# Second attention of a two-layer GNN/MoE kernel: ring buffers for the edge lists, the largest score by TensorE and VectorE, and the next stage's row statistics inside it

## The chip, the cores and the metric

One core of a Trainium2 chip runs the whole program. The metric is the device time of one execution in microseconds; the median of several runs is given. The engines are named as in the profile: PE (TensorE matmuls), PEld (its weight loads), DVE (VectorE), ACT (ScalarE), POOL (GpSimd) and SP (SyncE, here only a queue that issues DMAs). Each engine runs its own program; they meet at semaphores.

## The reference

x is 6250 rows of 256 columns, and there are 100,000 edges (src, dst) sorted by dst. Four stages add to x in turn, each on a layernorm of x:

```python
x = x + _L0_gnn_ref(_layernorm(x), edge_index, ...)      # first attention, one edge for each row
x = x + _L0_ffn_ref(_layernorm(x)[None], ...)[0]         # MoE, 6 experts, top 2
x = x + _L1_gnn_ref(_layernorm(x), edge_index, ...)      # second attention (GAT), 4 heads of 64
x = x + _L1_ffn_ref(_layernorm(x)[None], ...)[0]         # MoE, 8 experts, hidden 1024, top 2
```

The second attention, where most of the change is, computes for every edge and self-loop

```python
h = (x @ W).reshape(n, HEADS, OUT_C)
e = a_src[src] + a_dst[dst]
e = jnp.where(e > 0, e, NEG_SLOPE * e)
ex = jnp.exp(e - m[dst])                       # m: largest e of the destination
alpha = ex / (segment_sum(ex, dst)[dst] + 1e-16)
out = relu(segment_sum(alpha[:, :, None] * h[src], dst) + bias)
```

The kernel subtracts a bound instead of m: leaky_relu(largest a_src of all rows + a_dst of the row), which gives the same quotient. The second MoE's gate takes logits of the normalized rows, the two largest of 8, and a softmax over the two.

## The kernel before

The 6250 rows are 49 tiles of 128 (`TILES`), and x stays in SBUF (`K.X`). The stages follow each other, each in its own Blocks (a Block starts and ends with a barrier of all engines):

- `project` with tag a1: layernorm, first attention's part and router of the first MoE; its tokens are scattered into slots, 7 trips of 7 tiles (`TRIPS`, `BODY`). It stands at 100 to 420 us. A stage e0 computes the first MoE's experts, and b0, again `project`, combines and projects h and the scores for the second attention (`K.AD` holds a_src and a_dst of every row, `K.T1` in DRAM the rows h and a_src).
- `attention`: 865 to 2429 us.
- `project` with `gate`, tag b1: 2429 to 2627 us. Per trip of 7 tiles: `update` makes bn_stats (L793) and bn_aggr (L797) on DVE; `deviations` Sqrt on ACT (L926); `norm` the reciprocal and seven scalings (L812); PE transposes (L993), ACT copies (L959, L962), PE logits (L1004); `place` on DVE finds the two experts and, with PE's counts (`count`, L1026 to L1031, `ranks`), the slots (L860 to L880); POOL scatters 14 times into the slots (L691). POOL fills `token` and a column of `pad` with iota (L668, L670) at its start, and DVE copies the tokens (L737).
- e1, the second MoE's experts, to the end.

**The attention.** A first Block takes the largest a_src: DVE reduces over tiles (L1594 to L1597), POOL over partitions (`partition_all_reduce`, L1610), DVE makes the bound `adm` and the self-loops' exponents (L1599 to L1605), ACT takes Exp (L1615). The second Block walks 49 tiles of destinations; each has one or more steps of 17 x 128 = 2176 edges, some fifty steps in all, numbered s. A step's edges are three groups j of 6, 6 and 5 chunks of 128 (`CHUNKS`). For each group:

- SP loads the sources (`idx[j]`, L1685) once `scored[j]` says that DVE has used the gathered rows, and the destinations (`dcol[j]`, L1687) once `onehots[j]` is up; one load of `own` per tile (L1676). Loads of 24 or 20 bytes for each partition; the order on SP is idx0, dcol0, idx1, dcol1, idx2, dcol2.
- POOL waits for `src_in[j]` and for `agg_done[j]` of the step before, then issues one indirect gather for each chunk (L1700) of 128 rows into `G[j]`: 6, 6, 5 instructions.
- DVE compares the destinations with the tile's numbers: one-hots `OH[j]` (L1711). PE turns them (`turn`, L1836), ACT copies them to SBUF (`keep_turned`, L1809), PE multiplies them by the destinations' scores (`destinations`, L1844), DVE adds and rectifies (`scores`, L1720 to L1724), ACT takes Exp twice (`exps`, L1815, L1816), DVE weighs the rows (`weigh`, L1731), PE sums them into the tile (`aggregate`, L1851, `agg_done[j]`).

The order on each engine is written out. PE in a step: turn 0, turn 1, destinations 0, 1, (wait `acc_done`), aggregate 0, turn 2, destinations 2, aggregate 1, aggregate 2. ACT: keep_turned 0, 1, exps 0, keep_turned 2, exps 1, exps 2. DVE: one_hots 0, 1, scores 0, weigh 0, `absorb` of the step before (L1749), at a tile's end `finalize` (L1753 to L1760: divide, bias, relu, add to x), start of the next ACC (L1775, L1778), one_hots 2, scores 1, weigh 1, scores 2, weigh 2.

`lift` raises a semaphore by one at the start, so that `freed(eng, sem, n)`, a wait for n+1, passes for the first use. `Chain` is DVE's own order: `link` waits for the instruction before, `mark` only counts, `settle` waits for all.

## Time and profile before

| | us |
|---|---|
| runs | 3304.72, 3318.38, 3322.56 |
| median | 3318.38 |
| profiled execution | 3312.67, its span 3310.6 |
| second attention, share of the span | 1547 (47%) |
| b1 | 198 (6%) |
| a1, e0 with b0, e1 | 320, 440, 683 |
| busy over the span: PE, DVE, POOL, ACT | 2159, 1549, 1487, 1006 |
| mean granted clock of PE | 0.77 |

A profile row of a timeline gives the start in us from the span's start, the busy time, engine, line and operation, the tiles written and read, and in brackets the engine's idle time before it with what ended that. "remote" is an event whose origin the trace doesn't name, "issue" none that it shows. Busy time of POOL for an indirect DMA is the issuing; the transfer goes on behind it. The times of PE's ends are modelled. The column of rows named waits sums idle time by what ended it: total, number, longest.

### The profile page before, as it was taken

How to read it: one execution, taken by the hardware profiler on the slowest of the kernel's cores; microseconds unless marked ns; L12 is line 12 of the kernel's file. 1: busy time of each engine (PE TensorE's matmuls, PEld its weight loads, DVE VectorE, ACT ScalarE, POOL GpSimd, SP SyncE). 2: the span in 40 equal slices, each digit the busy share in tenths (PEclk: the TensorE clock that was granted, in tenths of full speed). 3: DMA queues.
4: the chain of work that ended last, by engine and by line, in shares of the span. 5: the costliest groups of instructions: out<-in, count | busy, mean ns of one | idle time of the engine just before them, and what ended most of it. 6: DMA issues, size and time to landing. Idle time of an engine off the chain costs nothing. (4 is left out here: it accounts for less than half of the span.)

```text
span 3310.6 us, 55683 instructions
## 1 busy us (share of the span) xinstructions
PE 2158.7 (65%) x13130; PEld 1965.5 (59%) x13131; DVE 1548.6 (47%) x4163; ACT 1006.1 (30%) x2712; POOL 1486.7 (45%) x1459
## 2 busy tenths in 40 slices
PE   6232259984466655656755656655654299999997
PEld 4132258873355554555654555555543299999997
DVE  5564435657334433433433433433445345556454
ACT  3132246663210111111111111111134266665664
POOL 1456634440255555555555545545525524334233
PEclk9655579997667767766767767767755599999999
DMA  6212233325333233233223323323333423333331
GB/s 177 62 55 66 73 114 106 110 93 188 93 82 78 76 79 79 76 79 78 76 79 78 79 73 79 79 77 80 79 98 125 137 42 89 46 66 85 48 68 25
DMA packets 232367, 279.34 MB, mean 84 GB/s; under 512 B 102963, under 2 KB 186526, under 8 KB 232086
## 3 DMA queue, kind: packets, MB, share of 16 engines
q0 software_dynamic: 82160, 200.19, 22.9%
q1 hardware_dynamic: 149392, 77.86, 9.0%
q10 hardware_dynamic: 776, 0.89, 0.1%
q14 instruction: 30, 0.25, 0.0%
q8 instruction: 9, 0.15, 0.0%
HBM read 202.11 MB, written 78.46 MB: 85 GB/s over the span
## 5 line engine op out<-in xcount | busy, mean ns | idle before, releaser
L1700 POOL DMA_INDIRECT at_G<-h_as,at_idx x850 | 805.9, 948 | 735.2 <-issue 385.5
L1851 PE MATMUL at_pAgg<-at_G,at_OH 128*128 128x260 f32 x1700 | 504.6, 462 | 91.8 <-DVE at_ACC L1749 51.0
L1851 PEld LDWEIGHTS at_pAgg<-at_G,at_OH 128*128 128x128 f32 x1700 | 387.6, 235 | 176.6 <-issue 51.3
L1836 PE MATMUL at_pTr<-g_ident,at_OH 128*128 128x128 f32 x850 | 157.1, 332 | 477.7 <-ACT at_OT L1809 436.9
L1809 ACT ACTIVATE at_OT<-at_pTr 128x384 f32<-128x384 f32 (+1 forms) x300 | 131.4, 471 | 1102.8 <-remote 695.3
L1836 PEld LDWEIGHTS at_pTr<-g_ident,at_OH 128*128 128x128 f32 x850 | 120.9, 170 | 513.7 <-ACT at_OT L1809 448.7
L1415 ACT ACTIVATE e_full<-e_pH,g_bias_hidden 128x256 f32<-128x256 f32 x640 | 322.6, 504 | 96.4 <-PE e_pH L1320 60.7
L1223 POOL DMA_INDIRECT out_dram<-e_ob,e_to x108 | 171.0, 1584 | 401.9 <-DMA out_dram<-e_ob,e_to 190.8
L1844 PEld LDWEIGHTS at_pAd<-at_cur,at_OT 128*128 128x128 f32 x1700 | 320.4, 290 | 49.8 <-ACT at_OT L1809 49.8
L1720 DVE TENSOR_TENSOR at_Z<-at_G,at_pAd 128x24 f32<-128x24 f32 x150 | 26.1, 174 | 690.0 <-PE at_pAd L1844 592.0
L1844 PE MATMUL at_pAd<-at_cur,at_OT 128*128 128x8 f32 x1700 | 319.1, 326 | 37.9 <-ACT at_OT L1809 37.9
L1731 DVE TENSOR_TENSOR at_G<-at_G,at_pIds 128x1536 f32<-128x1536 f32 x150 | 249.8, 1666 | 151.4 <-ACT at_pIds L1816 97.2
L1318 PE MATMUL e_pH<-e_xT_high,e_WA_high 128*128 128x256 f32 x1072 | 308.8, 288 | 7.6 <-DVE e_WA_low L1491 4.8
L1496 DVE TENSOR_TENSOR e_hT_low<-e_full,e_hT_high 128x256 fp32r<-128x256 f32 x536 | 260.0, 498 | 108.9 <-ACT e_hT_high L1416 107.4
L1319 PE MATMUL e_pH<-e_xT_low,e_WA_high 128*128 128x256 f32 x1072 | 303.3, 283 | 0.0
L1320 PE MATMUL e_pH<-e_xT_high,e_WA_low 128*128 128x256 f32 x1072 | 303.0, 283 | 0.0
L1416 ACT ACTIVATE e_hT_high<-e_pH,g_bias_hidden 128x256 fp32r<-128x256 f32 x536 | 275.3, 514 | 0.0
L1318 PE MATMUL e_pO<-e_WL_high,e_hT_high 128*128 128x256 f32 x864 | 250.0, 289 | 5.2 <-POOL e_WL_low L1247 3.4
L1319 PE MATMUL e_pO<-e_WL_low,e_hT_high 128*128 128x256 f32 x864 | 244.1, 283 | 0.0
L1320 PE MATMUL e_pO<-e_WL_high,e_hT_low 128*128 128x256 f32 x864 | 243.9, 282 | 0.0
L1318 PEld LDWEIGHTS e_pH<-e_xT_high,e_WA_high 128*128 128x128 f32 x1072 | 204.0, 190 | 12.1 <-issue 8.5
L1319 PEld LDWEIGHTS e_pH<-e_xT_low,e_WA_high 128*128 128x128 f32 x1072 | 204.5, 191 | 0.0
(307 smaller groups left out, 4089.3 us busy)
## 6 DMA issues: line engine op xcount, KB each, us to landing
e_xs<-slot_rows_e SPq DMA_DIRECT2D x55, 261.0 KB
e_xs<-slot_rows_e SPq DMA_DIRECT2D x54, 257.0 KB
at_G<-h_as,at_idx POOLq DMA_INDIRECT x850
b_rows<-expert_out SPq DMA_DIRECT2D x14, 896.0 KB, 7.3
g_raw_first<-in_L_ffn_W_dram POOLq DMA_DIRECT2D x8, 1024.0 KB, 8.1
g_raw_last<-in_L_ffn_W_dram POOLq DMA_DIRECT2D x8, 1024.0 KB, 6.3
xt_ar<-a_og SPq DMA_DIRECT2D x7, 910.0 KB, 4.5
h_as<-b_og SPq DMA_DIRECT2D x7, 910.0 KB
```

The source lines that it names most:

```text
L1223: gp.indirect_dma_start(K.out, at, ob[b][:, s, :], None, bounds_check=NODES - 1, oob_is_err=False, compute_op=ALU.add).then_inc(sent[s], 16)
L1318: nc.tensor.matmul(out, left[0], right[0], start=start, stop=False)
L1319: nc.tensor.matmul(out, left[0], right[1], start=False, stop=False)
L1320: return nc.tensor.matmul(out, left[1], right[0], start=False, stop=stop)
L1415: nc.scalar.activation(full[n][:, :], pH[n][:, 0:MT], func, bias=at)
L1416: nc.scalar.activation(to[b][0][:, u, :], pH[n][:, 0:MT], func, bias=at).then_inc(h_done, 1)
L1496: V.tensor_tensor(to[b][1][:, u, :], full[base + u % RING][:, :], to[b][0][:, u, :], ALU.subtract).then_inc(l_done, 1)
L1700: gp.indirect_dma_start(G[j][:, c, :], None, K.T1, bass.IndirectOffsetOnAxis(ap=idx[j][:, c:c + 1], axis=0)).then_inc(gathered[j], 16)
L1731: V.tensor_tensor(rows, rows, ex, ALU.mult).then_inc(msg_ready, 1)
L1836: last = nc.tensor.transpose(pTr[h][:, (c - a) * P:(c - a + 1) * P], OH[j][:, c, :], K.ident[:, :])
L1844: last = nc.tensor.matmul(pAd[j][:, 8 * c:8 * c + 8], OT[j][:, c, :], cur[:, :], start=True, stop=True)
L1851: last = nc.tensor.matmul(pAgg[:, 0:DIM + 4], OH[j][:, c, :], G[j][:, c, :], start=(j == 0 and c == 0), stop=(j == NJ - 1 and c == CHUNKS[ ...
```

## The change

1. **Attention.** The two Blocks become one. The maximum over partitions is made without POOL: PE turns `gm` (128 x 4), DVE reduces it to four numbers (`top`) and spreads them on a 4 x 4 diagonal (`each`), PE multiplies a matrix of ones by it, DVE copies the result. `maxima()` runs on DVE ahead of tile 0, ACT takes the self-loops' Exp in the same Block. Edge lists: one load for sources and one for destinations for each step (68 bytes for each partition, all 17 chunks) into rings of four steps (`edge_src`, `edge_dst`, `DEPTH`); SP waits for the slot to be free, and for both loads to land before the next step. `own` is a ring of four as well. ACT copies a group's sources from the ring to `idx[j]` (`keep_sources`), behind `exps(s, j)` for the next step, and POOL waits for `src_kept[j]` in place of `src_in[j]`. DVE reads the destinations from the ring. `finalize` also makes bn_stats and bn_aggr of the finished rows and keeps mean and variance of all tiles in `K.MV`.
2. **b1.** `update` does nothing; one Sqrt and one reciprocal over all 49 tiles stand at the start, and `norm` reads `K.MV` and `rstd` by tile.
3. **a1 and b1.** POOL's two iotas go; tokens are made once at the kernel's setup (`K.token`), and DVE derives the pad column.

```diff
 @@ project @@
-                nc.gpsimd.iota(token[:, :], pattern=[[P, TILES]], base=0, channel_multiplier=1,
-                               allow_small_or_imprecise_dtypes=True).then_inc(token_made, 1)
...
-                    v.wait_ge(token_made, 1)
-                    nc.vector.tensor_copy(Y[:, :, TO], token[:, :]).then_inc(consts, 1)
-
+                    nc.vector.tensor_copy(Y[:, :, TO], K.token[:, :]).then_inc(consts, 1)
...
                 def update(i):
 
+                    if gate:
+                        return
...
-                    v.wait_ge(std_ready, i + 1)
-                    nc.vector.reciprocal(rstd[:, :, :], std[:, :, :]).then_inc(rstd_ready, 1)
-                    v.wait_ge(rstd_ready, i + 1)
+                    if not gate or (isinstance(i, int) and i == 0):
+                        v.wait_ge(std_ready, i + 1)
+                        nc.vector.reciprocal(rstd[:, :, :], std[:, :, :]).then_inc(rstd_ready, 1)
+                        v.wait_ge(rstd_ready, i + 1)
...
-                        if j == BODY - 2:
+                        if j == BODY - 2 and not gate:
 @@ attention, SP @@
-                            freed(sp, scored[j], s)
-                            sp.dma_start(idx[j][:, :], K.SRCP[bass.ds(at[j], ne)].rearrange("(p c) -> p c", p=P)).then_inc(src_in[j], 16)
-                            freed(sp, onehots[j], s)
-                            sp.dma_start(dcol[j][:, :], K.DSTP[bass.ds(at[j], ne)].rearrange("(p c) -> p c", p=P)).then_inc(dst_in[j], 16)
+                        slot = sp.snap(s % DEPTH)
+                        landed = sp.snap(s * 16 + 16)
+                        sp.wait_ge(src_kept[NJ - 1], s + 1)
+                        sp.sem_inc(passed, 1)
+                        sp.dma_start(edge_src[:, bass.ds(slot, 1), :].rearrange("p o c -> p (o c)"),
+                                     K.SRCP[bass.ds(e0, SE)].rearrange("(p c) -> p c", p=P)).then_inc(src_in, 16)
+                        sp.wait_ge(onehots[NJ - 1], s + 1)
+                        sp.sem_inc(passed, 1)
+                        sp.dma_start(edge_dst[:, bass.ds(slot, 1), :].rearrange("p o c -> p (o c)"),
+                                     K.DSTP[bass.ds(e0, SE)].rearrange("(p c) -> p c", p=P)).then_inc(dst_in, 16)
+                        sp.wait_ge(src_in, landed)
+                        sp.wait_ge(dst_in, landed)
+                        sp.sem_inc(passed, 1)
 @@ attention, POOL @@
-                        gp.wait_ge(src_in[j], s * 16 + 16)
+                        gp.wait_ge(src_kept[j], s + (1 + (DEPTH if j == NJ - 1 else 0)))
                         freed(gp, agg_done[j], s)
 @@ attention, DVE: finalize @@
-                    ch.mark(V.scalar_tensor_tensor(Xt, res[:, :], 0.0, Xt, ALU.max, ALU.add))
+                    ch.link(V.scalar_tensor_tensor(Xt, res[:, :], 0.0, Xt, ALU.max, ALU.add))
+                    v.sem_inc(passed, 1)
+                    ch.link(V.bn_stats(stats[:, :], Xt))
+                    v.sem_inc(passed, 1)
+                    ch.link(V.bn_aggr(mean_var[:, :], stats[:, :]))
+                    ch.mark(V.tensor_copy(K.MV[:, bass.ds(t, 1), :].rearrange("p o k -> p (o k)"), mean_var[:, :]))
 @@ attention, DVE: maxima @@
+                    V.tensor_tensor(gm[:, :], gm[:, :], gt[:, :], ALU.max).then_inc(gm_ready, 1)
+                    v.wait_ge(gm_turned, 1)
+                    ch.link(V.tensor_reduce(top[:, :], pAgg[0:HEADS, 0:P], AX.X, ALU.max))
+                    V.tensor_scalar(each[:, :], K.ident[0:HEADS, 0:HEADS], top[:, 0:1], None, ALU.mult).then_inc(each_ready, 1)
+                    v.wait_ge(gm_all, 1)
+                    ch.link(V.tensor_copy(gt[:, :], pAgg[:, P:P + HEADS]))
 @@ attention, ACT @@
+                for j in J:
+                    keep_sources(0, j)
+                act.wait_ge(self_z, 1)
+                nc.scalar.activation(exs[:, :, :], exs[:, :, :], ACT.Exp).then_inc(exs_ready, 1)
...
                     keep_turned(s, 0)
                     keep_turned(s, 1)
                     exps(s, 0)
+                    keep_sources(ahead, 0)
                     keep_turned(s, 2)
                     exps(s, 1)
+                    keep_sources(ahead, 1)
                     exps(s, 2)
+                    keep_sources(ahead, 2)
 @@ attention, PE @@
+                pe.wait_ge(gm_ready, 1)
+                nc.tensor.transpose(pAgg[0:HEADS, 0:P], gm[:, :], K.ident[:, :]).then_inc(gm_turned, 1)
+                pe.wait_ge(each_ready, 1)
+                nc.tensor.matmul(pAgg[:, P:P + HEADS], allones[:, :], each[:, :], start=True, stop=True).then_inc(gm_all, 1)
```

`keep_sources(s, j)` waits for `src_in` of the step and is one ACT copy of 6 or 5 columns from the ring to `idx[j]`.

## Rows read from the trace of the kernel before

**Rows 1.** Windows by stage: us, busy (instructions) of PE, PEld, DVE, ACT, POOL, clock, DMA, GB/s.

```profile
882.00:2429.00 1547.00, 960.29 (x4250) 827.56 (x4248) 622.42 (x1388) 171.27 (x600) 805.06 (x850) 0.71 0.30 78
2429.00:2627.00 198.00, 67.56 (x351) 60.65 (x351) 84.35 (x403) 62.28 (x133) 96.83 (x102) 0.50 0.40 127
```

**Rows 2.** Waits in 1000 to 2200 us: total, times, longest.

```profile
ACT at_OT L1809 <- remote: 542.2, 41, 14.4
...
POOL at_G L1700 <- DMA at_idx<-src_padded: 162.6, 23, 7.4
POOL at_G L1700 <- PE at_pAgg L1851: 111.7, 15, 11.3
```

**Rows 3.** Timeline of one attention step, from one first gather to the next.

```profile
1029.67 0.95 POOL L1700 DMA_INDIRECT at_G<-h_as,at_idx  x1 [7.05 <-PE at_pAgg L1851]
...
1031.95 5.09 PE L1851 MATMUL at_pAgg<-at_G,at_OH 128*128 128x260 f32 x22 [0.70 <-DVE at_G L1731]
...
1037.30 0.87 PE L1836 MATMUL at_pTr<-g_ident,at_OH 128*128 128x128 f32 x6 [0.26 <-issue]
...
1043.44 0.94 POOL L1700 DMA_INDIRECT at_G<-h_as,at_idx  x1 [0.30 <-issue]
1046.73 0.87 ACT L1809 ACTIVATE at_OT<-at_pTr 128x384 f32<-128x384 f32 x2 [13.79 <-remote]
...
1047.45 0.94 POOL L1700 DMA_INDIRECT at_G<-h_as,at_idx  x1 [3.06 <-issue]
...
1054.74 4.79 PE L1851 MATMUL at_pAgg<-at_G,at_OH 128*128 128x260 f32 x12 [1.00 <-DVE at_ACC L1749]
...
1057.15 0.82 DVE L1711 TENSOR_TENSOR at_OH<-at_dcol,at_pIds 128x640 f32<-128x640 f32 x1 [0.22 <-DVE at_ACC L1778]
...
1059.37 0.71 PE L1836 MATMUL at_pTr<-g_ident,at_OH 128*128 128x128 f32 x5
...
1060.37 0.95 POOL L1700 DMA_INDIRECT at_G<-h_as,at_idx  x1 [6.97 <-PE at_pAgg L1851]
```

**Rows 4.** Timeline of the attention's start.

```profile
871.65 0.26 DVE L1599 COPY at_adm<-g_as_ad 128x196 f32<-128x196 f32 x1 [5.26 <-POOL at_gt L1610]
...
874.88 0.29 DVE L1791 TENSOR_SCALAR at_pIds<-g_iota 128x128 f32<-128x128 f32 x1 [0.69 <-PEq L1588]
...
881.19 1.19 POOL L1700 DMA_INDIRECT at_G<-h_as,at_idx  x1 [9.58 <-issue]
...
905.32 0.77 ACT L1809 ACTIVATE at_OT<-at_pTr 128x384 f32<-128x384 f32 x2 [13.54 <-remote]
```

**Rows 5.** Timeline of b1's start.

```profile
2429.22 1.28 ACT L926 ACT_TABLE_LOAD   x1 [6.64 <-PEq L1667]
...
2437.75 0.21 DVE L737 COPY b_Y<-b_token 128x49 f32<-128x49 f32 x1 [7.30 <-POOL b_token L668]
...
2438.14 2.39 DVE L793 BATCH_NORM_STATS2 b_stats<-g_x 128x6 f32<-128x256 f32 x7
...
2440.68 0.58 DVE L797 BATCH_NORM_AGGREGATE b_mv<-b_stats 128x2 f32<-128x6 f32 x7 [0.15 <-DVE b_stats L793]
...
2441.87 2.35 DVE L812 TENSOR_SCALAR b_yg<-g_x,b_mv,b_rstd 128x256 f32<-128x256 f32 x7
...
2450.93 1.28 ACT L959 ACT_TABLE_LOAD   x1
```

**Rows 6.** Timeline of b1's loop, second and last stream of scatters.

```profile
2483.24 0.22 DVE L860 TENSOR_TENSOR b_rank<-b_pr,b_region 128x56 f32<-128x56 f32 x1 [8.18 <-remote]
...
2486.59 0.97 POOL L691 DMA_INDIRECT slot_rows_e<-b_Y,g_slot_of  x1 [5.51 <-DVE g_slot_of L880]
...
2491.95 2.38 DVE L812 TENSOR_SCALAR b_yg<-g_x,b_mv,b_rstd 128x256 f32 x7 [1.99 <-issue]
...
2584.72 0.22 DVE L860 TENSOR_TENSOR b_rank<-b_pr,b_region 128x56 f32<-128x56 f32 x1 [0.55 <-PE b_pr L1031]
```

**Rows 7.** Timeline of POOL in a1: the scatter behind a pair of trips.

```profile
272.50 0.99 POOL L691 DMA_INDIRECT slot_rows_e<-a_Y,g_slot_of  x1 [7.04 <-DVE g_slot_of L880]
```

More of the change, by code:

```diff
@@ L41 @@
 CHUNKS = (6, 6, 5)
-OFFS = (0, 6 * P, 12 * P)
+OFFS = (0, 6, 12)
+ALL = sum(CHUNKS)
+DEPTH = 4
 SE = sum(CHUNKS) * P
@@ L397, in project @@
         stats = sb("stats", [P, BODY, 6])
-        mv = sb("mv", [P, BODY, 2])
-        std = sb("std", [P, BODY, 1])
-        rstd = sb("rstd", [P, BODY, 1])
+        n_std = TILES if gate else BODY
+        mv = K.MV if gate else sb("mv", [P, BODY, 2])
+        std = sb("std", [P, n_std, 1])
+        rstd = sb("rstd", [P, n_std, 1])
         yg = sb("yg", [P, BODY, DIM])
@@ L733, in _ @@
                         for e in range(2):
-                            last = nc.vector.memset(pad[:, e, :, part], 0.0)
-                    last.then_inc(pad_made, 1)
-                    v.wait_ge(token_made, 1)
-                    nc.vector.tensor_copy(Y[:, :, TO], token[:, :]).then_inc(consts, 1)
+                            nc.vector.memset(pad[:, e, :, part], 0.0)
+                    nc.vector.tensor_scalar(pad[:, :, :, TO].rearrange("p e s -> p (e s)"), K.token[:, 0:2 * SUB],
+                                            float(2 * NODEROWS if router else NODEROWS), None, ALU.add).then_inc(pad_made, 1)
+                    nc.vector.tensor_copy(Y[:, :, TO], K.token[:, :]).then_inc(consts, 1)
                     nc.vector.tensor_scalar(rev[:, :], K.iota[:, 0:E], -1.0, float(E), ALU.mult, ALU.add).then_inc(consts, 1)
@@ L924, in deviations @@
                         nc.scalar.activation(z[:, :, :], z[:, :, :], ACT.Exp).then_inc(exps_done, 1)
-                    act.wait_ge(stats_ready, i + 1)
+                    if not gate:
+                        act.wait_ge(stats_ready, i + 1)
                     nc.scalar.activation(std[:, :, :], mv[:, :, 1:2], ACT.Sqrt, bias=K.eps[:, 0:1]).then_inc(std_ready, 1)
@@ L1581, in attention @@
         gt = sb("gt", [P, HEADS])
+        top = sb("top", [HEADS, 1])
+        each = sb("each", [HEADS, HEADS])
+        allones = sb("allones", [HEADS, P])
         adm = sb("adm", [P, TILES, 8])
@@ L1622, in attention @@
         Z = [sb(f"Z{j}", [P, CHUNKS[j], HEADS]) for j in J]
-        own = sb("own", [P, DIM + 4])
+        own = sb("own", [P, DEPTH, DIM + 4])
         cur = sb("cur", [P, 8])
@@ L1657, in attention @@
         NJ = len(CHUNKS)
-        lifts = (own_used, acc_done, ot_ready, *scored, *onehots, *agg_done)
-        START, STEP, END = 2, 3 * NJ, 5
+        lifts = (acc_done, ot_ready, *scored, *onehots[0:NJ - 1], *agg_done)
+        START, STEP, END = 2, 3 * NJ, 8
+        stats = sb("stats", [P, 6])
+        mean_var = sb("mean_var", [P, 2])
         def tile_steps(eng, t):
@@ L1772, in tile @@
                         finalize(ch, t - 1)
+                    own_t = own[:, bass.ds(t % DEPTH if isinstance(t, int) else v.snap(t % DEPTH), 1), 0:DIM].rearrange("p o c -> p (o c)")
                     ex_t = exs[:, bass.ds(t, 1), :].rearrange("p o h -> p (o h)")
@@ L1789, in tile @@
                             assert cs.n == STEP
+                v.sem_inc(own_used, DEPTH)
+                v.sem_inc(onehots[NJ - 1], DEPTH)
+                maxima()
                 V.tensor_scalar(TI, K.iota[:, 0:P], -float(P), None, ALU.add).then_inc(init, 1)
@@ L1817, in exps, with keep_sources @@
                                          ACT.Exp).then_inc(ex_ready, 1)
+                def keep_sources(s, j):
+                    slot = act.snap(s % DEPTH) if not isinstance(s, int) else s % DEPTH
+                    act.wait_ge(src_in, s * 16 + 16)
+                    act.sem_inc(passed, 1)
+                    nc.scalar.activation(idx[j][:, :], edge_src[:, bass.ds(slot, 1), OFFS[j]:OFFS[j] + CHUNKS[j]].rearrange("p o c -> p (o c)"),
+                                         ACT.Copy).then_inc(src_kept[j], 1)
+                act.sem_inc(src_kept[NJ - 1], DEPTH)
+                for j in J:
+                    keep_sources(0, j)
+                act.wait_ge(self_z, 1)
+                nc.scalar.activation(exs[:, :, :], exs[:, :, :], ACT.Exp).then_inc(exs_ready, 1)
                 n, s0 = tile_steps(act, TILES - 1)
-                with act.Fori(0, act.snap(s0 + n)) as s:
+                total = act.snap(s0 + n)
+                with act.Fori(0, total) as s:
+                    ahead = act.snap(s + 1)
                     keep_turned(s, 0)
@@ L1830, in turn @@
                 def turn(s, j):
-                    freed(pe, onehots[j], s + 1)
+                    pe.wait_ge(onehots[j], s + (2 if j < NJ - 1 else 1 + DEPTH))
                     for h, (a, z) in enumerate(((0, 3), (3, CHUNKS[j]))):
```

102 lines of the change are left out of this document (54 added, 48 removed).

## The prediction

> **What bounds the kernel now.** I read the windows by stage first. The second attention takes 1547 of 3310 us, and in it no engine is full: PE 960, POOL 805, DVE 622, ACT 171 us [rows 1]. So a loop of waits bounds it, and the next view is the list of waits over forty of its steps [rows 2]. The largest entry is ACT's: 41 waits of 13 us each for "remote" in front of the OT copy. POOL's own long pauses are 23 that end with the index load (162.6 us) and 15 with PE's aggregation (111.7 us).
>
> The timeline of one step tells what lies behind them [rows 3]. POOL issues twelve gathers (groups 0 and 1), the last at 1043.44 for 0.94. PE ended the transposes that ACT wants at 1037.30+0.87=1038.17, yet ACT's OT copy starts only at 1046.73: 8.6 us after PE's end and 2.35 us after POOL's stream. POOL goes on with group 2 at 1047.45, also for something that PE had long ended. So **PE's completions reach nobody while POOL streams software DMAs**, from some 7 us into a stream until 2.3 us after it. In the stream of five that follows, handovers are prompt. From the release the path runs: ACT 1046.73, PE, DVE's scores and weighing, PE's aggregation of group 0 from 1054.74 to 1059.53, POOL's gather of the next step at 1060.37. Twelve gathers of 1.25 and the tail of 2.3 (17 us) bring the next release. The first gathers of two steps stand at 1029.67 and 1060.37, 30.70 us apart; fifty such steps are the stage.
>
> The gate and projection in front of the second MoE (b1, 198 us [rows 1]) has the same trait: POOL scatters 14 at a time by 1.27 us, DVE's rank addition L860 at 2483.24 waits 8.18 us for "remote", and the next scatter is at 2486.59 after a pause of 5.51 [rows 6].
>
> **The change part by part.** The sum is made against the profiled run, 3312.67 us (span 3310.6 and 2.1 around it); the median of the runs is 5.7 above it.
>
> (1) *Maximum without POOL, one Block instead of two.* Before, DVE idles 5.26 us for POOL's reduction; the second Block's first DVE instruction is at 874.88, the first gather 6.3 later at 881.19 [rows 4]. After, the index load starts with the Block (865.6) and needs nothing of DVE: 865.6+6.3, and 0.6 for ACT's copy, is 872.5, nearly 9 earlier. But the seven additions (0.36 to 0.40 each in the old order) and two handovers through PE bring DVE to the first one-hots some 3.5 us after the gathers. PE's first aggregation then falls over 7 us into a first stream of 17 gathers (21 us), and is likely held to its end, as ACT's wait of 13.54 us at 905.32, in this very step, was [rows 4]. So of the 9 us some 5 are given back. I take -4; bounds -9 (nothing held) and +3 (all of step 0 behind the stream).
>
> (2) *Rings of four, one load for three.* SP's waits for `scored` and `onehots` leave the path of the indices; ACT, busy 171 of 1547 us [rows 1], copies them. The tempting reading is that the 23 pauses that end with the index load go. They don't: with the load named a pause is 162.6/23=7.07 us, with PE named, its longest taken out, (111.7-11.3)/14=7.17 us [rows 2]. Both conditions come true within a few tenths of each other. PE's aggregation ends 0.84 before the gather, and POOL needed 0.72 from a release (ACT's start at 1046.73) to its gather at 1047.45 [rows 3]: what is late next is PE, by 0.1 to 0.2 us. I take 0.15 us for 48 steps and 3 for the one long pause: -10. Bounds 0, and 0.5 for each step, -25. Half of the index descriptors go, but no row shows a full DMA queue: nothing for it. Slots modulo four cost register steps on SP, ACT and DVE; DVE's are counted in (3).
>
> (3) *Row statistics in `finalize`, once per tile.* One more link behind L1760, bn_stats of 256 columns (2.39/7=0.34), bn_aggr (0.58/7=0.08 in a row of seven [rows 5]; linked about 0.2, an estimate from DVE's small operations) and a copy of 0.17, with semaphores and slot arithmetic: 1.1 us (0.8 to 1.5). Queued behind them on DVE are ACC's start, group 2's one-hots (1057.15+0.82=1057.97) and group 1's scores. PE turns group 2 at 1059.37, behind its twelve aggregation matmuls [rows 3], so 1.2 to 1.4 us are free: cost nothing, 49 times. If that cover is gone, PE's groups 1 and 2 come later, and behind them lie the 9 us in which results are held anyway. Only the last tile pays in the open: +0.8 at the stage's end.
>
> (4) *b1's start.* DVE waits 7.30 us for POOL's iota, then makes 2.39+0.58 of statistics; after ACT's Sqrt norm starts at 2441.87 [rows 5]. After the change nothing of POOL is in front: ACT's table load from 2429.22 to 2430.50, one Sqrt of 49 columns, a reciprocal, norm at about 2431.5: -10.4. In trip 0 ACT's detour (a table load of 1.28, a Sqrt of 0.3, and the load back at 2450.93 [rows 5]) goes too: -2.9. The first scatter comes 13.3 earlier; with (3)'s 0.8 taken off, -12.5. Bounds -9 (the gate's weights or bias land last) and -14.
>
> (5) *b1's loop.* Without statistics norm begins about 0.6 instead of 5.4 us into a stream of scatters (2491.95 against 2486.59 [rows 6]), and the count's matmuls about 7.2 us into it. The last trip shows what may be had: it has no norm ahead, L860 goes at 2584.72, 7.3 us into its stream, after 0.55 us of waiting [rows 6], and POOL scatters 28 without a pause. If each trip does so, five pauses of 5.0 to 5.5 us go: -26. But 7.2 is just where holding begins, and in a stream that runs on, transposes and logits of the next trip are held as well. The first router stage shows what comes then: two trips merged into one stream and a pause of 7.04 behind the pair [rows 7]. Five pauses of 5.3 against three of some 6.2: -8. Bounds 0 and -26.
>
> (6) *Iotas of a1 and setup.* Setup makes the tokens once, beside loads; in a1 DVE, not POOL's first gather, is late. Nothing.
>
> Sum: -4 -10 -12.5 -8 = -34.5, 3278 on the profiled run. The runs' median is 5.7 higher, of which I carry most: **3282 us**.
>
> Two rules of the Trainium skill are against this. GPSIMD Engine Reference, 4.1 Engine selection, gives a reduction along the partition dimension to GPSIMD and not to VectorE; by it, part (1) would cost its two handovers through PE, +1 instead of -4, and the total would be 3287. The wait of 5.26 us in front of L1599 speaks against the rule for one reduction of four columns. SBUF — State Buffer, Who interferes with whom, says that PE and ACT never wait on anyone and that DMA does not contend with a compute engine; ACT's 13.79 us for results that were complete 8.6 us before speaks of something that the page doesn't treat. By that rule part (5) would give its whole -26, total 3264.
>
> **The rivals.**
> *A, the label at its face*: the index load is what POOL waits for; in 49 steps 29 pauses of 7.07 us vanish, -205: 3087. Against it stands the equal length of the pauses that end with PE. 3%.
> *B, the rhythm flips*: group 1's aggregation ends about 5.2 us into the stream of twelve (12 of the 22 matmuls from 1031.95 [rows 3]). If its completion is held, POOL stops after six gathers, so the hold ends early (7.5+2.3), and it resumes with eleven; 13.7 us from that release to the next step, less what overlaps, makes a step of about 27.1: -3.6 for 49 steps, 3106. By the rows it takes 2 to 3 us of delay on DVE (L860 passed at 7.3, the transposes at 8.5 were held); I allow for one, and (3) adds 1.1 against 1.2 of slack. 9%.
> *C, b1 scatters without pauses*: -18 more, 3264. 22%.
> *D, little happens*: (1) gives +3, (2) and (5) nothing, (4) stays: -10, 3308 on the median. All three sit at the edge of the held time. 15%.
> *E, slower*: the statistics land on the path. The place is DVE between absorb L1749 and group 2's one-hots; from 1.2 us of added work on, PE's turn of group 2 and its aggregation of groups 1 and 2 move, and if the held time doesn't take this up, each tile pays what was added, 1.1 us, up to 1.9 with one more handover (0.8): 49 times, +54 to +93, 3336 to 3375. Against it: ACT's copies of group 2 and the next step's work come before a release that POOL alone sets. 8%.
> *F, the rings never run ahead*, since SP waits for both loads of a step before the next: (2) is nought, all else as forecast, 3292.
>
> **How the numbers follow.** The forecast has 43%, F among it, C 22, D 15, B 9, A 3, E 8. The range leaves out A, B and E, 20%: from C with (1) and (2) at better values (3264-5-15=3244, taken 3240) to D's 3308 with its rounding, 3312. A measurement of this kernel can tell about 0.5% (16.6 us) from no change. Faster: forecast, C, A, B, 0.77; same, D, 0.15; slower, E, 0.08.
>
> **What would show it.** In the new profile the first gathers of two steps stand 30.5 to 30.6 us apart (B: 27; E: over 31.5); POOL's pause before them is about 6.9 with PE named each time; ACT's waits of 13 to 14 us for "remote" are still there; PE's turn of group 2 still follows its twelve matmuls at once. The first gather is at 872 to 873, the second step's near 904. b1's first scatter comes 13 us sooner after attention's end, no Sqrt load stands in its loop, and POOL pauses fewer than five times. The prediction is wrong if a step's length changes by over 0.5 us either way, the only term with a factor of fifty.

## The result and the profile after

| | before | after |
|---|---|---|
| median of 6 runs each, us | 3315.3 | 3219.0 |
| range | 3304.7 to 3322.6 | 3203.9 to 3238.0 |
| profiled run, its span | 3312.7, 3310.6 | 3223.0, 3221.4 |
| mean granted clock of PE | 0.77 | 0.773 |

The ratio is 0.972, 95% interval 0.970 to 0.974: 96 us faster. The forecast was 3282, range 3240 to 3312; the direction was right and the gain nearly three times what was forecast.

Windows by stage of the changed kernel, in the columns of [rows 1]: second attention, then b1.

```profile
869.40:2353.20 1483.80, 1008.46 (x4250) 842.39 (x4250) 673.63 (x1539) 194.32 (x752) 813.83 (x850) 0.71 0.30 81
2353.20:2537.20 184.00, 67.81 (x351) 60.29 (x351) 62.62 (x300) 43.93 (x114) 98.04 (x100) 0.50 0.45 137
```

Attention takes 1484 us (869.4, its first gather, to 2353.2) and does the same work: POOL 814 us busy against 805. The 89 us between the two spans split as follows. The start of attention, read at the first gather of its second step, gives 4.4 (906.06 to 901.65). From there to the first gather of the last step it was 1482.8 us and is 1404.7: 78.1. The last step and the stage's end cost 6.6. The way from attention's end to b1's first scatter went from 34.3 to 22.3 us: 12.0. b1's scatters give 3.4, and what lies between them and e1 costs 2. So nearly all of the surprise is in the 48 steps between the second and the last, of 30.9 us before and 29.3 on average now.

Before, they were nearly equal (47 of 48 take 30.5 to 31.5 us). That is no longer so. Timeline of the changed kernel over two steps: the last of SP's loads first, then POOL's first gather of each pause and the work that answers to [rows 3] (turn is L1890, OT copy L1845, aggregation L1905).

```profile
1016.41 0.35 SPq L1662 DMA_DIRECT2D at_own<-h_as  x1
1017.40 0.34 SPq L1671 DMA_DIRECT2D at_edge_src<-src_padded  x1
...
1017.60 0.95 POOL L1701 DMA_INDIRECT at_G<-h_as,at_idx  x1 [11.12 <-PE at_pAgg L1905]
...
1020.73 5.09 PE L1905 MATMUL at_pAgg<-at_G,at_OH 128*128 128x260 f32 x22 [0.70 <-DVE at_G L1735]
...
1026.99 0.95 POOL L1701 DMA_INDIRECT at_G<-h_as,at_idx  x1 [2.13 <-issue]
...
1042.71 0.77 ACT L1845 ACTIVATE at_OT<-at_pTr 128x384 f32<-128x384 f32 x2 [11.69 <-remote]
...
1043.43 0.96 POOL L1701 DMA_INDIRECT at_G<-h_as,at_idx  x1 [2.88 <-issue]
...
1045.68 7.08 PE L1905 MATMUL at_pAgg<-at_G,at_OH 128*128 128x260 f32 x22
...
1051.37 0.95 POOL L1701 DMA_INDIRECT at_G<-h_as,at_idx  x1 [0.68 <-issue]
...
1060.56 0.87 ACT L1845 ACTIVATE at_OT<-at_pTr 128x384 f32<-128x384 f32 x2 [13.20 <-remote]
...
1068.15 0.42 DVE L1753 TENSOR_TENSOR at_ACC<-at_ACC,at_pAgg 128x260 f32<-128x260 f32 x1
...
1072.85 0.82 DVE L1715 TENSOR_TENSOR at_OH<-at_edge_dst,at_pIds 128x640 f32<-128x640 f32 x1 [0.30 <-DVE at_ACC L1811]
...
1074.84 0.95 POOL L1701 DMA_INDIRECT at_G<-h_as,at_idx  x1 [7.46 <-PE at_pAgg L1905]
```

The first step runs from 1017.60 to 1043.43, **25.8 us**. POOL stops after six gathers of group 0 (at +7.3) and waits 2.13 us, until +9.4. Group 1's aggregation was ready to tell by +6 (12 of the 22 matmuls from 1020.73), but reaches POOL only once POOL's stream has ended. In that pause everything PE held comes through, ACT and PE go on at once, and groups 1 and 2 follow as one stream of eleven. At its end, 2.2 us later, the OT copy (1042.71) and group 0's aggregation are released together, and the next step's gathers start at 1043.43 without the 7 us that stood there before. The second step, from 1043.43 to 1074.84, is of the old kind (31.4): group 1 is told of at +7.9, POOL idles 0.68, the stream of twelve runs to 1058.6, ACT waits for its end, and the pause of 7.46 before the next first gather is back. Of 48 steps 22 are short (25.9 us on average), 14 take 29 to 32 us and 12 take 33 to 35. Only 6 of the 26 long ones are of the old kind, at 31 to 32 us.

The other 20, from 28.6 to 35.0 us, are a third kind. POOL's first gathers of groups 0, 1, 2 in the last step of the changed kernel:

```profile
2306.39 0.95 POOL L1701 DMA_INDIRECT at_G<-h_as,at_idx  x1 [12.22 <-PE at_pAgg L1905]
...
2314.33 0.95 POOL L1701 DMA_INDIRECT at_G<-h_as,at_idx  x1 [0.68 <-issue]
...
2322.18 0.96 POOL L1701 DMA_INDIRECT at_G<-h_as,at_idx  x1 [0.59 <-issue]
```

Here group 2 found its condition true in the middle of the stream (pause 0.59), POOL ran 17 gathers with no rest of even 1 us, and all that PE owed the other engines came late. The step before it, from 2272.41, has the same pauses (0.62 and 0.64) and took 34.0 us.

### The profile page after: what moved, and what is told of

Read it like the earlier page. It is cut to its first block and busy times, and to the rows that moved or that the text cites. A ratio compares the mean times of both kernels' runs of the same rounds, so it can differ in the third digit from the quotient of the medians.

```text
span 3221.4 us, 56679 instructions
## 1 busy us (share of the span) xinstructions
PE 2203.0 (68%) x13133; PEld 1975.8 (61%) x13134; DVE 1577.0 (49%) x4212; ACT 1010.1 (31%) x2846; POOL 1493.4 (46%) x1455
## 3 DMA queue, kind: packets, MB, share of 16 engines
q0 software_dynamic: 82160, 200.19, 23.2%
## 5 line engine op out<-in xcount | busy, mean ns | idle before, releaser
L1905 PE MATMUL at_pAgg<-at_G,at_OH 128*128 128x260 f32 x1700 | 592.4, 524 | 154.0 <-DVE at_ACC L1753 84.7
L1905 PEld LDWEIGHTS at_pAgg<-at_G,at_OH 128*128 128x128 f32 x1700 | 448.4, 270 | 260.8 <-DVE at_G L1735 127.7
L1845 ACT ACTIVATE at_OT<-at_pTr 128x384 f32<-128x384 f32 (+1 forms) x300 | 130.4, 471 | 999.0 <-remote 522.4
L1898 PE MATMUL at_pAd<-at_cur,at_OT 128*128 128x8 f32 x1700 | 293.9, 309 | 133.2 <-ACT at_OT L1845 118.3
L1898 PEld LDWEIGHTS at_pAd<-at_cur,at_OT 128*128 128x128 f32 x1700 | 290.2, 264 | 147.1 <-ACT at_OT L1845 130.1
L1890 PE MATMUL at_pTr<-g_ident,at_OH 128*128 128x128 f32 x850 | 144.4, 307 | 188.9 <-ACT at_OT L1845 94.9
L1890 PEld LDWEIGHTS at_pTr<-g_ident,at_OH 128*128 128x128 f32 x850 | 107.0, 156 | 234.0 <-issue 119.9
```

The source lines that it names most:

```text
L1890: last = nc.tensor.transpose(pTr[h][:, (c - a) * P:(c - a + 1) * P], OH[j][:, c, :], K.ident[:, :])
L1898: last = nc.tensor.matmul(pAd[j][:, 8 * c:8 * c + 8], OT[j][:, c, :], cur[:, :], start=True, stop=True)
L1905: last = nc.tensor.matmul(pAgg[:, 0:DIM + 4], OH[j][:, c, :], G[j][:, c, :], start=(j == 0 and c == 0), stop=(j == NJ - 1 and c == CHUNKS[ ...
```

## The experiments

The experiments ran on four chips. On two of them the kernel before takes 3333 us, and PE's completions are held back while POOL streams, as the prediction describes; this is called the hold below. On the two others it takes 2783 us, and the traces show no hold at all. Ratios are always to the kernel before on the same chip. The diffs are excerpts.

**Statistics alone, in the kernel before.**

```diff
-                    ch.mark(V.scalar_tensor_tensor(Xt, res[:, :], 0.0, Xt, ALU.max, ALU.add))
+                    ch.link(V.scalar_tensor_tensor(Xt, res[:, :], 0.0, Xt, ALU.max, ALU.add))
...
+                    ch.link(V.bn_stats(stats[:, :], Xt))
...
+                    ch.link(V.bn_aggr(mean_var[:, :], stats[:, :]))
+                    ch.mark(V.tensor_copy(kept[:, bass.ds(t, 1), :].rearrange("p o k -> p (o k)"), mean_var[:, :]))
```

> The kernel before with one addition: finalize also makes bn_stats, bn_aggr and a copy on DVE for each tile, whose result nobody reads (b1 still makes its own). Theory 1 (the added DVE work shifts group 1's aggregation past the point from which PE's completions are held, POOL then stops after six gathers and the hold ends early): the steps alternate between about 25.9 and 31 to 33 us as in the changed kernel, and the run is 50 to 80 us faster than before although it only has more work. Theory 2 (the rings and the fewer loads make the short steps): steps stay at 30.8 us, the time is that of before plus 0 to 2 us.

Measured: 3408.5 against 3333.4, ratio 1.023 (1.021 to 1.025). Slower, with 45 of 48 steps at 32 to 33 us and no short one. Both theories fall: the statistics alone do not make short steps, and they cost 1.5 us a step. Timeline of one step end:

```profile
1172.54 0.42 DVE L1783 TENSOR_TENSOR at_ACC<-at_own,at_exs 128x256 f32<-128x256 f32 x1
...
1173.15 0.34 SPq L1679 DMA_DIRECT2D at_own<-h_as  x1
...
1173.89 0.33 SPq L1688 DMA_DIRECT2D at_idx<-src_padded  x1
...
1174.24 0.75 PE L1844 MATMUL at_pTr<-g_ident,at_OH 128*128 128x128 f32 x5
...
1176.44 0.94 POOL L1703 DMA_INDIRECT at_G<-h_as,at_idx  x1 [8.41 <-DMA at_idx<-src_padded]
```

ACC's start (L1783) comes behind the statistics; own's load waits for it, the index load stands behind own's load on SP, and POOL's gather waits for the index load, 8.41 us instead of 6.97 [rows 3]. PE's turn of group 2 (1174.24) waits for nothing new.

**The change without its statistics.** `finalize` and b1 as before; rings, maximum and iotas as changed.

> The changed kernel with the statistics taken back to b1 (update, Sqrt and reciprocal for each trip as before); rings, the maximum without POOL and the iotas stay as changed. Theory 1: steps of 30.5 to 30.7 us, and against before only the start of attention (-4), some of the loop (-5 to -10) and b1's start without the iota (-7): 3295 to 3302 where before has 3315. Theory 2: the alternation of 25.9 and 31 to 33 us is still there, about 3235.

Measured: 3177.8 against 3333.4, ratio 0.954 (0.951 to 0.958), on the chip of the first experiment. Theory 1 falls, theory 2 stands: short steps need no statistics, and of the rest of the change only the rings are in the loop. Of 48 steps 32 are short, the mean is 28.1 us. SP's load, then POOL's first gathers, in one of them (the next step begins at 1183.87):

```profile
1156.84 0.01 SPq L1669 DMA_DIRECT2D at_edge_src<-src_padded  x1
...
1157.81 0.95 POOL L1699 DMA_INDIRECT at_G<-h_as,at_idx  x1 [2.87 <-issue]
...
1167.19 0.95 POOL L1699 DMA_INDIRECT at_G<-h_as,at_idx  x1 [2.15 <-issue]
```

**One wait more.** In the changed kernel, and for itself in the kernel before:

```diff
                        freed(gp, agg_done[j], s)
                        gp.sem_inc(passed, 1)
+                        if j == 1:
+                            freed(gp, agg_done[2], s)
+                            gp.sem_inc(passed, 1)
```

> The changed kernel with one wait more: before group 1's gathers POOL waits for group 2's aggregation of the step before as well (it had to wait for it before group 2 anyway). Theory 1: POOL now pauses after six gathers in every step, PE's completions come through there, and the two groups behind it run as one stream of eleven; the short step of 25.9 to 26.5 us becomes the rule, 49 times 2.5 to 3 us less than the changed kernel's mean of 29.2: 3219-130=3090, range 3070 to 3120. Theory 2 and any theory in which a wait costs POOL time: a step is longer by the pause of 1 to 2 us, 3219+50=3270 or more.

> The kernel before with the same one wait more and nothing else of the change. Theory 1: steps of 25.9 to 26.5 us, or up to 0.8 more where the index loads now come last, 49 times 4 to 4.9 less: 3315-220=3095, range 3075 to 3150. Theory 2: as before or slower by 1 to 2 us for each step, 3315 to 3400.

Measured: 3134.9, ratio 0.940 (0.937 to 0.943), and 3144.7, ratio 0.942 (0.940 to 0.945). The added wait alone, without any of the change, is worth 5.8%, more than the change in any of its runs (2.8 to 4.9%). In either kernel nearly every step is 27.3 us; POOL's first gathers in one of the changed kernel:

```profile
1138.40 0.95 POOL L1704 DMA_INDIRECT at_G<-h_as,at_idx  x1 [2.82 <-issue]
...
1149.06 0.95 POOL L1704 DMA_INDIRECT at_G<-h_as,at_idx  x1 [3.41 <-PE at_pAgg L1908]
```

The pause behind the sixth gather is 3.4 us, since group 2's aggregation ends last, and the step ends with a pause of 2.9 (the next one begins at 1165.73) where the old one had 7. The expected 3090 was too low by 45, mainly because group 1 starts at +10.7 and not at +9.4. Since the kernel before, with its own loads, gets the same steps, the pause is enough, whatever SP's loads do.

**Own's ring under the statistics.** The first experiment with own in a ring of four and nothing else of the change (SP's side; DVE reads the same slot):

```diff
-                    freed(sp, own_used, t)
-                    sp.dma_start(own[:, :], K.T1[bass.ds(r0, P), :]).then_inc(own_in, 16)
+                    place = sp.snap(t % 4)
+                    sp.wait_ge(own_used, t + 1)
+                    sp.sem_inc(passed, 1)
+                    sp.dma_start(own[:, bass.ds(place, 1), :].rearrange("p o c -> p (o c)"), K.T1[bass.ds(r0, P), :]).then_inc(own_in, 16)
```

> The kernel before with the unused row statistics of the first experiment and, from the change, only the ring of four for own (so that SP loads own before ACC's start of the tile before has used the last one). In the first experiment the pause before the first gather ended with the index load, which stands on SP behind own's load, which waits for ACC's start, which stands on DVE behind the statistics. Theory P (that chain is what the statistics cost): with the chain cut the 32.4 us steps fall to 30.8 us or below, the time is 3325 to 3340 where before has 3333. Rival Q (the statistics cost by PE's and DVE's work coming later, whatever SP does): steps stay at 32.3 us, about 3408.

This run fell on the chip without the hold: 2786.1 against 2783.3, ratio 1.002 (1.000 to 1.004), steps of 21.4 us. List of waits over 37 of its steps:

```profile
ACT at_OT L1821 <- PE at_pTr L1848: 506.6, 112, 8.5
```

ACT's OT copy waits only for the transposes themselves, no entry names "remote", and POOL's gaps are the 0.30 us between two gathers: 17 gathers of 1.25 us are the step. That chip tells nothing of theory P. The kernel was run again elsewhere:

> As for the run of the same kernel before, which fell on a chip without the hold and so told nothing of it (there ratio 1.002). On a chip with the hold: theory P (the statistics cost because own's load and then the index load stand behind them) 30.8 us steps or less, ratio 0.97 to 1.002; rival Q (they cost by later PE and DVE work) 32.3 us steps, ratio 1.02.

Measured: 3283.3 against 3333.6, ratio 0.986 (0.983 to 0.990). Theory P holds: with the chain through SP cut, the statistics cost nothing, 33 of 48 steps take 30.7 to 31.6 us, and 12 take 26 or 27 us. In 4 of the 12 POOL stops for 2.1 to 2.2 us behind the sixth gather, as in the changed kernel, so such steps also come without the rings of the edge lists. POOL's first gathers around one:

```profile
1094.31 0.94 POOL L1705 DMA_INDIRECT at_G<-h_as,at_idx  x1 [6.83 <-PE at_pAgg L1863]
...
1103.66 0.94 POOL L1705 DMA_INDIRECT at_G<-h_as,at_idx  x1 [2.17 <-issue]
...
1120.25 0.94 POOL L1705 DMA_INDIRECT at_G<-h_as,at_idx  x1 [3.14 <-remote]
```

**A wait for the landed rows.**

```diff
+                        if j == 1:
+                            gp.wait_ge(gathered[0], s * (16 * CHUNKS[0]) + 16 * CHUNKS[0])
+                            gp.sem_inc(passed, 1)
```

> The changed kernel with one other wait: before group 1's gathers POOL waits until its own six gathers of group 0 have landed (about 2 us after the last). Theory 1 (any pause of POOL behind the sixth gather that is long enough to let PE's completions through gives the short step): group 1 starts 9.4 to 9.6 us after the first gather in every step, steps of 26.0 to 26.3 us, 1 us shorter than with the wait for group 2's aggregation, where POOL went on at +10.7: 3135-50=3085 on this count, range 3070 to 3110. Rival R (what helps is that group 2's aggregation is in before group 1 starts, not the pause): the streams of 11 become streams of 11 with a pause or of 17, steps of 29 us and more, 3200 or above.

> As for the run of the same kernel before, which on a chip without the hold made each step 2.4 us longer (23.8 us, ratio 1.036), the price of the pause itself. On a chip with the hold: theory 1, steps of 26.0 to 26.3 us, ratio 0.925; rival R, 29 us and more, ratio 0.965 or above.

On the chip without the hold: 2885.0 against 2783.3, ratio 1.036 (1.034 to 1.038), 23.8 us a step; the pause is pure loss there. On a chip with it: 3097.5 against 3333.6, ratio 0.931 (0.927 to 0.934), steps of 26.5 us:

```profile
1096.26 0.95 POOL L1704 DMA_INDIRECT at_G<-h_as,at_idx  x1 [3.12 <-issue]
...
1106.13 0.96 POOL L1704 DMA_INDIRECT at_G<-h_as,at_idx  x1 [2.62 <-DMA at_G<-h_as,at_idx]
```

This is the fastest version measured on a chip with the hold, 236 us below the kernel before, 96 us (by ratio 0.931 against 0.956) below the changed kernel on the same chip. The next step begins at 1122.76. Theory 1's part on the pause stands, rival R falls.

**SP's loads moved.** The kernel without statistics, with SP's three loads held until DVE has issued group 2's weighing (`v.sem_inc(past, 1)` behind it):

```diff
                    sp.wait_ge(own_used, t + 1)
...
+                    sp.wait_ge(past, s0 + 1)
...
                        sp.wait_ge(src_kept[NJ - 1], s + 1)
...
+                        sp.wait_ge(past, s + 1)
```

> The kernel of the second experiment (rings, no statistics in attention) with SP's three loads of a step (own, sources, destinations) held until DVE has issued the weighing of group 2, so that they are issued about 4 us into the stream or in POOL's pause, not in the 3 us before the first gather. Theory S (loads issued by SP just before the stream make the hold of PE's completions begin early, at 5 to 6 us instead of after 7, and so make the short steps): nearly all steps are 30.6 us, 3178 + 50 x 2.5 = 3300. Rival T (the loads have no part in it; the time at which PE ends group 1's aggregation decides): steps as in the second experiment, 26.0 in most, mean 28.1, about 3180.

> As for the run of the same kernel before (rings, no statistics, SP's loads kept out of the last 3 us before the stream), which fell on a chip without the hold (ratio 0.996). On a chip with the hold: theory S (loads just before the stream make the hold begin early) nearly all steps 30.6 us, ratio 0.99; rival T, steps as in the second experiment, ratio 0.954.

Without the hold: 2771.9, ratio 0.996 (0.994 to 0.998). With it: 3307.6 against 3333.6, ratio 0.991 (0.988 to 0.994), and 45 of 48 steps at 30.7 to 31.4 us. SP's loads and POOL's first gathers in one step:

```profile
1099.96 0.02 SPq L1663 DMA_DIRECT2D at_own<-h_as  x1
1105.02 0.70 SPq L1674 DMA_DIRECT2D at_edge_src<-src_padded  x1
1108.58 0.70 SPq L1678 DMA_DIRECT2D at_edge_dst<-dst_padded  x1
...
1095.79 0.95 POOL L1704 DMA_INDIRECT at_G<-h_as,at_idx  x1 [6.82 <-PE at_pAgg L1905]
...
1113.84 0.95 POOL L1704 DMA_INDIRECT at_G<-h_as,at_idx  x1 [3.25 <-issue]
```

The loads come 4 to 13 us into the stream, and POOL stops only once, before group 2. So SP's loads have a part in the short steps, as theory S said. The experiment alone doesn't exclude rival T, for with late loads PE also ends group 1's aggregation earlier than in most short steps. Steps of the kernel without statistics in which PE keeps the same times decide that:

```profile
1480.52 0.34 SPq L1669 DMA_DIRECT2D at_edge_src<-src_padded  x1
...
1482.28 0.95 POOL L1699 DMA_INDIRECT at_G<-h_as,at_idx  x1 [6.75 <-PE at_pAgg L1898]
...
1484.63 5.09 PE L1898 MATMUL at_pAgg<-at_G,at_OH 128*128 128x260 f32 x22 [0.70 <-DVE at_G L1733]
...
1491.75 0.95 POOL L1699 DMA_INDIRECT at_G<-h_as,at_idx  x1 [2.23 <-issue]
...
2230.03 0.95 POOL L1699 DMA_INDIRECT at_G<-h_as,at_idx  x1 [6.52 <-PE at_pAgg L1898]
...
2232.39 5.09 PE L1898 MATMUL at_pAgg<-at_G,at_OH 128*128 128x260 f32 x22 [0.70 <-DVE at_G L1733]
...
2237.57 0.95 POOL L1699 DMA_INDIRECT at_G<-h_as,at_idx  x1 [0.30 <-issue]
```

In both, PE's aggregation starts 2.4 us after the first gather and takes 5.09. In the first, SP's loads stand 2.8 to 1.2 us before the stream, and POOL waits 2.23 us; in the second there is none in the last 3.5 us, and POOL goes on after 0.30. All four steps of the first kind in this trace were held, all three of the second were not.

But the loads are not the whole trigger. In the changed kernel's trace 22 steps have the sources' load 0.7 to 1.1 us before the stream; in 4 of them POOL waited over 2 us for group 1, in 18 it went on within 1.4 us. The step at 1043.43 above is one of the 18 (its load at 1042.58, pause 0.68). In the kernel with only own's ring the short step at 1094.31 had no load in the 7 us before it. And the kernel before issued its index loads 1.1 to 2.7 us before the first gather and had no short step. Own's load isn't needed: in the step at 1157.81 it stood 6.6 us before the stream. What in the loads does it is open. Two kernels were to tell the edge loads from own's:

> Rings, no statistics, and only the two edge loads of a step held until DVE has issued the weighing of group 2; own's load as in the change. Theory S1 (the edge loads 1 us before the stream make the early hold): steps of 30.7 us in most, ratio 0.985 to 0.995. Rival S2 (own's load does it): short steps stay in more than half, ratio 0.95 to 0.965. On a chip without the hold both give 0.995 to 1.0 and tell nothing.

> Rings, no statistics, and only own's load held until DVE has issued the weighing of group 2; edge loads as in the change, though SP reaches them only behind own's load. Theory S1: as SP then stands in own's wait while the stream begins, the edge loads too come after it, so steps of 30.7 us, ratio 0.985 to 0.995; if they still are 1 us before the stream, short steps and 0.955. Rival S2: 30.7 us steps wherever the edge loads are. The place of the loads in the trace, beside the steps, decides between the two.

Both fell on a chip without the hold (2772.0 and 2772.6 against 2782.7, ratios 0.996 and 0.996) and tell nothing of it.

**Gathers of 16 bytes.** The kernel before, gathering 4 columns in place of 260:

```diff
-                            gp.indirect_dma_start(G[j][:, c, :], None, K.T1,
+                            gp.indirect_dma_start(G[j][:, c, DIM:DIM + 4], None, K.T1.rearrange("n (a b) -> (n a) b", b=4),
...
+                for j in J:
+                    V.memset(G[j][:, :, 0:DIM], 0.0)
```

It leaves the messages out of the attention's result (their columns stay zero), and the index, counted in pieces of 16 bytes, no longer finds the source's scores.

> The kernel before with gathers of 4 columns (16 bytes for each partition) in place of 260; the message columns of G are zeros, so the second attention's sums are left out of the output, and POOL still issues 17 gathers for each step. Theory U (the hold comes from POOL's issuing): ACT's wait of 13 to 14 us for remote and steps of 30 to 31 us stay, time within 30 us of before. Rival V (it comes from the moving of the gathered rows, 133 KB for each gather): the hold is gone, the steps are bound by POOL at 22 to 26 us, time 3333-250 or less.

> The kernel before with gathers of 4 columns instead of 260 (the message columns are zeros, so the second attention's sums are left out), as in the run that fell on a chip without the hold and had ratio 1.000 there. On a chip with the hold: theory U (POOL's issuing holds the completions) steps stay at 30 to 31 us, ratio 0.99 to 1.01; rival V (the moved rows do it) steps of 21.3 to 25 us, ratio 0.86 to 0.92.

Without the hold: ratio 1.000 (0.999 to 1.001), 21.3 us a step. With it: 3331.8 against 3334.3, ratio 0.999 (0.997 to 1.001), 31.1 us a step. The page's row of POOL's queue and the first entry of the list of waits, on the chip with the hold:

```profile
q0 software_dynamic: 68560, 88.78, 12.0%
...
ACT at_OT L1811 <- remote: 549.9, 40, 14.5
```

88.78 MB are moved instead of 200.19, and ACT still waits 13.7 us in each step. Rival V falls: the hold goes with POOL's issuing and not with the gathered bytes. The number of packets, 68,560 against 82,160, fell by only a sixth, so its part isn't told apart from the issuing.

**Controls on one chip.**

> The changed kernel itself, as a control, since the chip of the last group of runs showed no hold at all (steps of 21.3 us, POOL-bound; before 2783 us). If this chip holds completions (before near 3320 to 3335): ratio 0.97 as on record. If it doesn't: steps of 21.4 us in both kernels, so the statistics and rings do nothing in the loop; only the starts of attention and b1 and b1's loop gain, about 8+12+7 us of 2783, ratio 0.99.

> The changed kernel as the control of the run above: ratio 0.956 to 0.972 on a chip with the hold, mean step 28.5 to 29.3 us, 20 to 60 us slower than the one without statistics by the frequency of long steps; 0.99 on a chip without the hold.

> The changed kernel with the statistics in b1, beside the changed kernel on the same chip. If the statistics only cost what they take on DVE and that is covered: the changed kernel is faster than this one by b1's statistics, 5 to 8 us. If they make steps of 31 to 34 us more frequent (the trace on record had 25 long ones of 48, the one without statistics 16): this one is 20 to 60 us faster than the changed kernel. I expect the latter.

> The changed kernel without statistics in attention and with POOL's wait for its own landed gathers before group 1. In a short step the statistics lie in a time in which DVE waits for the release anyway, so here they should be free: steps of 26.5 us as with them (ratio 0.931), plus b1's statistics and its Sqrt loads, 5 to 8 us: ratio 0.932 to 0.935. If the statistics do cost in each step, 26.0 us steps and ratio 0.925.

The changed kernel again: 0.956 (0.952 to 0.961) with 31 short steps of 48, and 0.951 (0.947 to 0.954) with 33; in the result above it was 0.972 with 22. Without statistics, beside the last: 0.957 (0.953 to 0.961), 29 short steps. My expectation that the statistics make it 20 to 60 us slower was wrong: the changed kernel is 26 us faster than the one without them. The same kernel moved by 24 us between its two groups on this chip, so the pair doesn't show a gain of the statistics either. With the pause and without statistics: 3102.9, 0.931 (0.927 to 0.934), the same as with them.

## Why the prediction was wrong

**The bound** was read rightly: completions are held while POOL streams and released 2.3 us after it. The small gathers confirm that POOL's issuing goes with it. What the profile of one chip could not show is that another chip does not hold them, with 21.3 us steps in the kernel of the small gathers and 2783 us for the kernel before.

**(1) The start** is right in size and working, its exact size by luck: the first gather came earlier by more than I took, and as much more was given back.

```profile
863.63 0.37 PE L1910 MATMUL at_pAgg<-g_ident,at_gm 128*4 128x128 f32 x1 [7.98 <-DVE at_gm L1779]
...
865.25 0.16 DVE L1784 COPY at_gt<-at_pAgg 128x4 f32<-128x4 f32 x1 [0.67 <-PE at_pAgg L1912]
...
869.37 0.99 POOL L1701 DMA_INDIRECT at_G<-h_as,at_idx  x1 [121.85 <-ACT at_idx L1860]
...
893.38 0.18 DVE L1724 TENSOR_TENSOR at_Z<-at_G,at_pAd 128x24 f32<-128x24 f32 x1 [18.47 <-remote]
...
901.65 0.95 POOL L1701 DMA_INDIRECT at_G<-h_as,at_idx  x1 [11.11 <-PE at_pAgg L1905]
```

The two handovers through PE take 1.6 us (863.63 to 865.25), the first gather comes at 869.37, 11.8 earlier instead of 9, PE's results are held to the stream's end (DVE waits 18.47 us), and the second step starts 4.4 us earlier against the 4 forecast.

**(2) The rings** are the step that failed: -10 us forecast, -78.1 measured. Its own claim, that the index load is only co-critical, holds: with SP's loads out of the way the rings bring steps from 30.89 to 30.74 us on average, near the 0.15 that I took (30.84 without one short step among them; the 30.89 is of another chip). But I counted the loads only by their waits and descriptors; that the place at which SP issues them could move the hold, and with it POOL's stops, stands nowhere in the term. With the new places PE's completion of group 1 is held in 22 to 33 of 48 steps, POOL stops after six gathers, and these steps take 26 us. In the profiled run 22 short steps give 110 us, the other 26, at 32.1 on average, take 32 back: 78 against 10. That the loads have a part is shown; why the hold begins earlier stays open.

**Rival B** had the mechanism (POOL stops after six, is released early, resumes with eleven) and nearly the length (27.1 against 25.8), but the wrong trigger and all or nothing. The 27.1 doesn't follow from the terms that it names, 9.8 and 13.7; the trace has 9.4 to the restart, 13.6 for eleven gathers and a pause of 2.9. I had it need 2 to 3 us of delay on DVE; the first experiment put 1.5 us there and got no flip, and the kernel without statistics flips without any. 9% for a case whose price was 180 us was the mistake in the range, too: the rhythm is one of several, and a kernel may share its steps between them.

**(3) The statistics** were mis-sized and rightly placed. From absorb to the end of group 2's one-hots it was 3.78 us [rows 3] and is now (1068.15 to 1073.67) 5.52: 1.7 us, not 1.1, above the slack of 1.2 that I allowed. It still costs nothing: with the pause for the landed rows the kernel has ratio 0.931 with the statistics and without, since in a short step DVE and PE wait for the release anyway, and with own's ring alone the long steps stay at 30.8 us. In the kernel before the same work would have cost 1.5 us a step, rival E's size and sign, by a way that I had not looked at: behind ACC's start stands SP, with own's load and then the index load. I named what is queued on DVE and not who waits for it on SP. Own's ring, of which the forecast said nothing, is enough to make the statistics free.

**(4) b1's start** is right: 12.0 us against 12.5.

```profile
2353.00 0.17 DVE L1769 COPY g_mean_var<-at_mean_var 128x2 f32<-128x2 f32 x1
...
2354.75 0.34 ACT L929 ACTIVATE b_std<-g_mean_var,g_eps 128x49 f32<-128x49 f32 x1
...
2355.70 2.65 DVE L813 TENSOR_SCALAR b_yg<-g_x,g_mean_var,b_rstd 128x256 f32<-128x256 f32 x7
...
2375.51 1.04 POOL L689 DMA_INDIRECT slot_rows_e<-b_Y,g_slot_of  x1 [19.21 <-ACT b_Y L965]
```

One Sqrt of 0.34 us over 49 columns, norm 2.7 us after the last row of attention is kept. The first scatter follows at 2375.51.

**(5) b1's loop** gave 3.4, with 8 forecast and 0 to 26 as bounds. The count ends 8.3 us into the stream, not 7.2, and is held:

```profile
2383.56 0.21 PE L1034 MATMUL b_pr<-b_before,g_ones 128*128 128x56 bf16 x1
...
2392.52 0.22 DVE L862 TENSOR_TENSOR b_rank<-b_pr,b_region 128x56 f32<-128x56 f32 x1 [9.26 <-remote]
...
2398.24 0.98 POOL L689 DMA_INDIRECT slot_rows_e<-b_Y,g_slot_of  x1 [5.07 <-ACT b_Y L965]
```

DVE's L862 waits 9.26 us, and the pause before the next scatter is 5.07 as before it was 5.51. All five pauses stayed, though two of them shrank to 4.3 and 2.1 us, and no two trips merged into one stream as forecast. By the rule of the Trainium skill that I had weighed (SBUF — State Buffer, Who interferes with whom: DMA does not contend with a compute engine) nothing would have been held here and the whole 26 us gained; the row speaks against reading it that far.

**The sum**: start of attention -4.4, its loop -78.1, its end +6.6, b1's start -12.0, b1's loop -3.4, the way to e1 +2.0, against -4, -10, 0, -12.5, -8, 0. Four of six terms are within 5 us.

## What to carry to other kernels

Where the trace shows completions that arrive only when one engine's stream of DMAs ends, treat the length of that stream as a size to tune: a pause put in on purpose behind the sixth gather (one wait) was worth 5.8% by itself and 6.9% together with the change, more than the change alone (2.8 to 4.9%). Test on more than one chip before shipping it: where the hold is absent, the changed kernel with the pause is 3.6% slower than the kernel before. The changed kernel by itself was not run there; its version without statistics and with late loads has ratio 0.996. When work is added on one engine, follow the wait across the queues that stand behind it (DVE, then SP's own load, then SP's index load, then POOL), not only down the same engine.

## What the runs showed of the hardware

- The same kernel before takes 3315 to 3334 us on some chips and 2783 on others. Most of the difference is the step of attention: 30.9 us in its trace with the hold, 21.3 and 21.4 us in the traces of two of its variants without; with the hold ACT waits 13 to 14 us a step for transposes that are done, without it no such wait is in the list.
- The hold goes with POOL's issuing and not with the bytes: 16 bytes for each partition and row instead of 1040 leave it as it is (31.1 us a step).
- The point from which it holds is not fixed: group 1's aggregation passed about 7 us into the stream in some steps and was held at 5 to 6 us in others. At equal times of PE it was held in the four steps with loads of SP up to 2.8 us before the stream and not in the three without. But steps with such loads were also passed, and a few without them held; what decides is open.
- One program on one chip falls into three kinds of steps, 26, 31 and 27 to 35 us. How many short ones there are (33, 31, 22 of 48) goes with the changed kernel's ratio (0.951, 0.956, 0.972).
